# The last chunk tile by tile, row factors spread one chunk earlier, and two reordered pieces of preparation in a one-core transformer block

## The reference

```
h = layernorm(x)
C_q  = h @ Wq_d + bq_d            # 1024 -> 12
C_kv = h @ Wkv_d + bkv_d          # 1024 -> 4
q = (C_q @ W_qk + b_qk) by head   # 32 heads of 4
attn = softmax(q . C_kv / sqrt(4))
V = C_kv @ Wv_u + bv_u            # 32 heads of 32
x = x + (attn @ V) @ Wo + bo
x = x + layernorm(x) @ W.T + bias + LoRA(layernorm(x))
```

## Time and profile before

| | us |
|---|---|
| median of 3 runs | 2104.05 |
| lowest, highest | 2103.58, 2106.32 |
| time of the profiled execution | 2106.0 |
| span of its trace, first to last instruction | 2104.2 |
| TensorE busy | 1966.4 |
| ScalarE busy | 1959.2 |
| VectorE busy | 491.6 |
| GpSimd busy | 215.7 |
| mean granted TensorE clock, share of full | 0.989 |

### The profile page before, as it was taken

How to read it: one execution, slowest core, us unless ns; L and a number is a source line. 1 busy time by engine, 2 the same in 40 slices (tenths; PEclk the granted TensorE clock), 3 DMA queues, 4 the chain that set the end, 5 groups by cost and what they waited for, 6 DMA issues and landing times. The chain is left out here.

```text
span 2104.2 us, 36028 instructions
## 1 busy us (share of the span) xinstructions
PE 1966.4 (93%) x15041; PEld 713.3 (34%) x15041; DVE 491.6 (23%) x1213; ACT 1959.2 (93%) x2161; POOL 215.7 (10%) x220
## 2 busy tenths in 40 slices
PE   6868898999999999999999999999999999999999
PEld 3412222333333333333333333333333333333337
DVE  7812342211121111211111111212111111212115
ACT  3678999999999999999999999999999999999970
POOL 4700000000100001100100001100110001100021
PEclk9979999999999999999999999999999999999999
DMA  8452000000010000100010000100010000100010
GB/s 297 146 142 83 5 25 25 3 15 25 25 34 4 25 25 13 35 15 25 25 33 5 25 26 13 35 15 25 13 45 5 25 13 26 35 15 15 24 41 40
DMA packets 45663, 77.42 MB, mean 37 GB/s; under 512 B 15871, under 2 KB 29751, under 8 KB 45499
## 3 DMA queue, kind: packets, MB, share of 16 engines
q1 hardware_dynamic: 45498, 75.11, 10.6%
HBM read 51.23 MB, written 23.86 MB: 36 GB/s over the span
## 5 line engine op out<-in xcount | busy, mean ns | idle before, releaser
L610 ACT ACTIVATE probs<-ps 128x1024 f32<-128x1024 f32 x2048 | 1899.9, 1029 | 25.5 <-PE ps L842 14.9
L853 PE MATMUL ps<-probs,c_wide 128*32 128x512 f32 x8192 | 989.8, 601 | 0.0
L842 PE MATMUL ps<-q_in,key_t 27*128 27x512 bf16 x4096 | 405.4, 386 | 96.3 <-ACT probs L610 92.3
L899 PE MATMUL ps<-w_eff,xn_t 128*128 128x512 f32 x1344 | 394.3, 418 | 0.0
L853 PEld LDWEIGHTS ps<-probs,c_wide 128*32 128x32 f32 x8192 | 212.8, 108 | 427.0 <-issue 221.4
L842 PEld LDWEIGHTS ps<-q_in,key_t 27*128 27x128 bf16 x4096 | 103.0, 91 | 728.0 <-ACT probs L610 716.0
L1346 DVE SCALAR_TENSOR_TENSOR y<-ps,nw,y 128x512 f32<-128x512 f32 x64 | 48.0, 750 | 976.3 <-PE ps L899 967.3
L899 PEld LDWEIGHTS ps<-w_eff,xn_t 128*128 128x128 f32 x1344 | 228.2, 188 | 101.8 <-issue 69.8
L529 POOL TENSOR_TENSOR y<-y,ffn_bias 128x1024 f32<-128x1024 f32 x32 | 76.4, 2387 | 1358.3 <-DVEq L1367 1358.3
L524 POOL TENSOR_TENSOR y<-y,attn_bias 128x1024 f32<-128x1024 f32 x32 | 75.7, 2382 | 469.6 <-DMA y<-in_L_attn_x_dram 469.5
L541 ACT ACTIVATE area<-ps 128x512 f32<-128x512 f32 x64 | 37.3, 615 | 45.8 <-PE ps L641 45.8
(11 more groups left out here) (154 smaller groups left out, 591.3 us busy)
## 6 DMA issues: line engine op xcount, KB each, us to landing
y<-in_L_attn_x_dram SPq DMA_DIRECT2D x40, 512.0 KB, 4.0
out_dram<-y SPq DMA_DIRECT2D x32, 512.0 KB, 2.7
area<-in_L_attn_x_dram SPq DMA_DIRECT2D x16, 512.0 KB, 7.7
q_in<-q_parts SPq DMA_DIRECT2D x256, 27.0 KB
q_parts<-q_parts_sb SPq DMA_DIRECT2D x48, 128.0 KB, 2.6
xn<-in_L_attn_x_dram SPq DMA_DIRECT2D x8, 512.0 KB, 4.9
y<-in_L_attn_Wo_dram SPq DMA_DIRECT2D x1, 2048.0 KB, 8.3
xn<-in_L_attn_Wo_dram SPq DMA_DIRECT2D x1, 2048.0 KB, 14.4
```

Of the source, the lines that this page charges most:

```text
L610: nc.scalar.activation(probs[:, (c * STEPS + step) % PROBS, bass.ts(pair, 2 * N)], ps[:, 2 * (i % SCORE_SLOTS):2 * (i % SCORE_SLOTS) + 2, ...
L842: last = nc.tensor.matmul(ps[:, at, :], key_t[TILE * h:TILE * h + KEYS, bass.ts(b * KT + kt, P)], q_in[TILE * h:TILE * h + KEYS, g % 2, :] ...
L853: last = nc.tensor.matmul(ps[32 * h:32 * h + 32, SUMS, :], c_wide[:, b * KT + kt, at:at + 32], probs[:, (c * STEPS + step) % PROBS, bass.t ...
L899: last = nc.tensor.matmul(ps[:, SHARED, :], xn_t[:, t % 2, a, kb, :], w_eff[:, b, kb, bass.ts(half, N)], start=(kb + i == 0), stop=(kb == ...
```

## The change

Four edits, in the order of the time in which they act.

1. `spread_r(c)` moves to the end of its own chunk: on TensorE behind `turn_x(c, 7)`, on ScalarE directly behind the move of turned block 7, ahead of the value and query moves of chunk c-1. The multiplication by it stays where it is.
2. For the last chunk the queries are made ahead of the turned latents, and ScalarE writes `q_abs` first, then the values, then the queries. For the other chunks the order inside is the old one.
3. `turn_lora(m)` waits for `prep_ok` of m - 1 instead of m. VectorE moves both halves of lora_b first, and only then fills `lv`, in 8 copies of 32x16 instead of 32 copies of 32x4, and `bv_wide`.
4. The last chunk goes tile by tile: ScalarE copies the four tiles of the sums, each is turned into a bank of its own, normalized, turned back into a bank of its own, its high part copied by ScalarE and its low part subtracted by VectorE. ScalarE also takes the high halves of the turned y. The statistics of a tile come behind its split, the dense layer waits for each half of the turned y by itself, and the last tile is stored in two halves.

```
         # TensorE, stage 1
-                    if kb == 0 and c:
-                        spread_r(c - 1)
...
                     if kb == 6 and c:
-                        use_latents(c - 1, (c - 1) % 2)
+                        turn_latents(c - 1, (c - 1) % 2)
+                        queries(c - 1)
+                    if kb == KB - 1:
+                        spread_r(c)
...
-            use_latents(CHUNKS - 1, 1)
+            queries(CHUNKS - 1)
+            turn_latents(CHUNKS - 1, 1)
         # ScalarE, stage 1
-                    if kb == 1 and c:
-                        move_r(c - 1)
                     if kb == 4 and c:
                         move_latents(c - 1, (c - 1) % 2)
+                    if kb == KB - 1:
+                        move_r(c)
                     if kb == KB - 1 and c:
-                        move_products(c - 1, (c - 1) % 2, (c - 1) // 2)
+                        move_values(c - 1)
+                        move_q(c - 1, (c - 1) % 2, (c - 1) // 2)
+                        move_q_abs(c - 1)
         # preparation
             def turn_lora(m):
-                free_bank(m)
+                free_bank(m - 1)
...
+            dve.wait_ge(prep_ok, 1)
+            for odd in range(2):
+                for h in range(4):
+                    at = 16 * odd + L * h
+                    nc.vector.tensor_copy(lv[32 * h:32 * h + 32, odd::2, at:at + L], wv_t[32 * h:32 * h + 32, odd::2, :])
         # last chunk, ScalarE
+            act.wait_ge(pv_done, CHUNKS * STEPS)
+            for t in range(TT):
+                nc.scalar.activation(o_sb[:, bass.ts(t, P)], ps[:, SUMS, bass.ts(t, P)], ACT.Copy).then_inc(last_o, 1)
+            for t in range(TT):
+                act.wait_ge(last_back, t + 1)
+                nc.scalar.activation(o_t[:, 0, bass.ts(t, P)], ps[:, BACK_BANK[t], 0:P], ACT.Copy).then_inc(last_high, 1)
+            for t in range(TT):
+                act.wait_ge(ffn_ready, START + (p * TT + max(t - 1, 0)) * 2)
+                for u in range(2):
+                    act.wait_ge(t_ready, START + CHUNKS * KB + (p * TT + t) * 2 + u + 1)
+                    nc.scalar.activation(xn_t[:, t % 2, 0, 4 * u:4 * u + 4, :].rearrange("p a n -> p (a n)"),
+                                         ps[:, 4 + u, :], ACT.Copy).then_inc(y_high, 1)
         # last chunk, TensorE
+            for t in range(TT):
+                pe.wait_ge(last_o, t + 1)
+                nc.tensor.transpose(ps[:, t, 0:P], o_sb[:, bass.ts(t, P)], ident[:, :]).then_inc(last_turned, 1)
...
+            back_last(0)
+            back_last(1)
             project_last(0)
+            back_last(2)
+            back_last(3)
             project_last(1)
             turn_last(0)
             project_last(2)
         # last chunk, VectorE (each step for one tile)
+            norm_last(0)
+            norm_last(1)
+            split_last(0)
+            norm_last(2)
+            split_last(1)
+            norm_last(3)
+            split_last(2)
+            split_last(3)
...
             for t in range(TT):
-                ch = Chain(v_ln)
-                residual(p, t, (2 * (t % 2), 2 * (t % 2) + 1), ch)
+                residual_last(t)
                 if t:
                     add_dense(p, t - 1, 0, 6)
-                move_xn(p, t, (4, 5))
+                low_last(t)
+                ch = Chain(v_ln)
+                dve.wait_ge(y_ready, START + (p * TT + t + 1) * 2)
+                measure(ch, y, t)
                 finish(ch, t)
```

More of the change, by code:

```diff
@@ L250, in build_block @@
         out_done = [sem(f"out_done{t}") for t in range(TT)]
+        last_o = sem("last_o")
+        last_turned = sem("last_turned")
+        last_rec = sem("last_rec")
+        last_normed = sem("last_normed")
+        last_back = sem("last_back")
+        last_high = sem("last_high")
+        last_low = sem("last_low")
+        y_high = sem("y_high")
         block = ctx.enter_context(nc.Block())
@@ L455, in _ @@
             beside_attention(CHUNKS - 1, False, True)
+            for t in range(TT - 1):
+                store_out(CHUNKS - 1, t)
+            for half in range(2):
+                sp.wait_ge(ffn_moved, START + CHUNKS * UNITS - 1 + half)
+                sp.dma_start(out_t[CHUNKS * TT - 1][:, half * N:(half + 1) * N], y[:, TT - 1, half * N:(half + 1) * N]
+                             ).then_inc(out_done[TT - 1], 16)
             for t in range(TT):
-                store_out(CHUNKS - 1, t)
-            for t in range(TT):
-                sp.wait_ge(out_done[t], CHUNKS * 16)
+                sp.wait_ge(out_done[t], (CHUNKS + t // (TT - 1)) * 16)
         @block.gpsimd
@@ L678, in use_latents, with queries @@
                 last.then_inc(caug_ps, 1)
+            def queries(c):
                 pe.wait_ge(q_read, START + c)
@@ L1007, in _ @@
                 for half in range(2):
-                    pe.wait_ge(t_moved, START + CHUNKS * KB + (p * TT + t + 1) * 2)
                     if t:
                         pe.wait_ge(ffn_moved, START + (p * TT + t) * 2 - 1 + half)
+                    else:
+                        pe.wait_ge(last_low, TT)
                     for kb in range(KB):
+                        if half == 0 and kb % 4 == 0:
+                            pe.wait_ge(t_moved, START + CHUNKS * KB + (p * TT + t) * 2 + kb // 4 + 1)
                         if half == 1 and kb == KB // 2 and t < TT - 1:
@@ L1257, in _ @@
             ch.end()
-            dve.wait_ge(prep_ok, 1)
-            for g in range(G4):
-                for h in range(4):
-                    at = 16 * (g % 2) + L * h
-                    nc.vector.tensor_copy(lv[32 * h:32 * h + 32, g, at:at + L], wv_t[32 * h:32 * h + 32, g, :])
-            nc.vector.tensor_copy(bv_wide[:, :, 0:1], bv_col.unsqueeze(2)).then_inc(prep_ok, 1)
             for half in range(2):
@@ L1268, in _ @@
                                         ALU.mult, ALU.mult).then_inc(prep_ok, 1)
+            dve.wait_ge(prep_ok, 1)
[3 more added lines that the diff above has]
+                    nc.vector.tensor_copy(lv[32 * h:32 * h + 32, odd::2, at:at + L], wv_t[32 * h:32 * h + 32, odd::2, :])
+            nc.vector.tensor_copy(bv_wide[:, :, 0:1], bv_col.unsqueeze(2)).then_inc(prep_ok, 1)
             ch = Chain(v_set)
@@ L1388, in _, with norm_last @@
             p = CHUNKS - 1
-            move_o(p, 1)
-            norm_o(p, 1)
-            split_o(p)
-            dve.wait_ge(t_ready, START + CHUNKS * KB + p * UNITS)
+            dve.wait_ge(o_back, START + p)
+            def norm_last(t):
+                dve.wait_ge(last_turned, t + 1)
+                turned = ps[:, t, 0:P].rearrange("p (h m) -> p h m", h=4)[:, :, 0:4 * W5].rearrange("p h (g d) -> p h g d", d=W5)
+                nc.vector.reciprocal(recip[:, t, :, :], turned[:, :, :, L]).then_inc(last_rec, 1)
+                dve.wait_ge(last_rec, t + 1)
+                nc.vector.tensor_tensor(o_q[:, t, 64:128].rearrange("p (g h d) -> p h g d", h=4, d=L),
+                                        turned[:, :, :, 0:L], recip[:, t, :, :].unsqueeze(3).to_broadcast([P, 4, 4, L]),
+                                        ALU.mult).then_inc(last_normed, 1)
@@ new lines, in split_last @@
+            def split_last(t):
+                dve.wait_ge(last_high, t + 1)
+                nc.vector.tensor_tensor(o_t[:, 1, bass.ts(t, P)], ps[:, BACK_BANK[t], 0:P],
+                                        o_t[:, 0, bass.ts(t, P)].bitcast(F32), ALU.subtract).then_inc(last_low, 1)
+            norm_last(0)
+            norm_last(1)
+            dve.wait_ge(proj_ready, START + p * UNITS)
+            split_last(0)
+            norm_last(2)
+            split_last(1)
+            norm_last(3)
```

47 lines of the change are left out of this document (32 added, 15 removed).

## The result

| | before | after |
|---|---|---|
| median, us | 2104.12 (4 runs, 2103.58 to 2106.32) | 2087.63 (4 runs, 2087.39 to 2088.13) |
| profiled execution, us | 2106.0 | 2087.39 |
| span of its trace, us | 2104.2 | 2085.6 |
| mean granted TensorE clock | 0.989 | 0.996 |
| ScalarE idle ahead of exponentials | 25.5 | 19.1 |

The ratio of after to before is 0.992, with an interval of 0.9903 to 0.9937. The change gains 16.5 us by the medians, where 12.3 was forecast: 4.2 us short, outside the forecast's own 2089.8 to 2094 and at the very edge of the wide range, where rival A stood (2087.5). The direction was right.

What follows compares the result with a forecast made beforehand. ScalarE's exponentials were taken as the bound, so only time before, in holes of, or after them counts. 2106.0 - 5.6 - 2.0 - 4.1 - 0.6 = 2093.7 us profiled; median 2104.05 - 12.3 = 2091.8, range 2087.5 to 2097.

Steps and rivals of the forecast that it cites:

- rival A: Stage 1: the cast does not wait for GpSimd as read; 4.0 us gained in place of +0.3, 2087.5 us; chance 0.15.
- Place 1, the turned lora_b: Around 168 us: turning lora_b ahead of the lv copies removes ScalarE's 3.39 and 2.18 us holes, -5.6 us.
- rival B: Around 168 us: lv is late because copies cost by elements; times_wo stalls 3.8 us, 2097.4 us; chance 0.07.
- Place 2, stage 1: Loop of scales: copying the row factors earlier gains nothing, scale(5) +0.3 us, between -0.7 and +1.2.
- the cast waits for GpSimd's last split operation: Stage 1: VectorE's latents cast ends about 0.3 us after GpSimd's last split operation; 1.2 us gained, 1.6 given back.
- From scale(2) on VectorE is late by itself, and copying the factors earlier gives it nothing: Stage 1: VectorE's own chain of waits sets the 10.15 us between scales, so earlier row factors gain nothing there.
- From stage 1 to the first scores: Between scale(7) and attention: earlier factors and queries bring weigh to 107.4 from 109.45, -2.0 us (bounds -1.0 and -3.0).
- Rival E: Attention's start: TensorE stays at half clock longer, making the kernel slower than before; chance 0.02.
- Place 3: Last chunk's start: tile-by-tile work at assumed half clock starts the dense layer at about 2047.6, -4.1 us; 5 at full clock.
- Inside the dense part finer waits give nothing: Last chunk's dense matmuls: TensorE was continuous there, so finer waits gain nothing.
- C: Stage 1: GpSimd sets every chunk's loop, 0.25 us longer each; attention starts where it did, 2093.8 us; chance 0.12.
- D: Last chunk: its small pieces are dear, 2 us gained in place of 4.1, 2093.9 us; chance 0.08.

Runs made afterwards that it cites:

- With the split left out: GpSimd's split of the queries left out (second and third bf16 parts zero), in edit 1 alone and in the kernel before: 2097.72 and 2104.35 us, one run each.
- With edit 1 and without the split: Edit 1 alone on the kernel before, with GpSimd's split of the queries left out: 2097.72 us, one run.
- with the spare matmuls alone: The kernel before with four spare matmuls on TensorE in the last chunk's start: 2103.56 us, ratio 0.9993 (0.9984 to 1.0002).
- the spare matmuls at the start: The changed kernel with nine spare 128x512 f32 matmuls around attention's start, results never read: 2086.30 us, again 2085.88 against 2088.50 for the changed kernel.

## Why the prediction was wrong

The bound was read rightly: nearly everything gained lies ahead of the first exponential, in a hole of their row, or behind the last one. What failed is the clock: TensorE's half clock at the start of attention and of the last chunk was carried over unchanged, and the hole that it makes behind the first exponentials had a term of 0. One reading of the rows was wrong too. "The rest lies ahead of 130 us" made some 14 us of the 25.5 into idle time there, and the timeline has 3.35, the two holes; the waits view of before puts only 14.9 down to the scores. These 3.35 us were given no place in the sum. The steps one by one:

- **Place 1, the turned lora_b: right.** -5.6 forecast and traced; alone it gave 6.2 by the medians. With the 5.7 us that attention is ahead there, the forecast's 169.9 for lv is 164.2, and it was ready at 163.8. The copies cost per instruction, and rival B was never near. The 2.18 us of its second hole scatter in the kernel before (0.96 to 2.18 over the traces), so a term of one execution carried more than the other traces have; that edit 3 alone still gave 6.2 is no contradiction, since its interval goes from 3.8 to 8.2 us, and its trace had a fuller clock as well.
- **Place 2, stage 1: wrong in sign, small.** "Scale(5) +0.3" was measured as -0.95, less than a third of the way from there to rival A's -4.0. The step that failed is "the cast waits for GpSimd's last split operation". It waits only for the one that is running, gets in ahead of the next, and the VectorE operation behind it then waits. From scale(1) to scale(2) it is 10.56 us, where I had 11.8, and scale(2) came at 53.46, not 54.1. Scale(1) itself gained 0.62 of the forecast 1.2 between the two traces, and the rest of that is not the edit's. The `down` matmuls at 35.7 us took 1.47 us in the first trace of before and 1.89 after; in the second trace of before, of unchanged code, they took 1.90, and scale(1) came at 43.94, 1.04 behind the 42.90 of after. The section "Who interferes with whom" of the Trainium skill's "SBUF — State Buffer" has the later instruction blocked while the other holds the port; the traces agree, with that holder being one instruction (0.28 us behind 43.90), and it was I who had made it three.
- **"From scale(2) on VectorE is late by itself, and copying the factors earlier gives it nothing": half right.** With the split left out, the factors' copy appears as the wait for every scale. Up to scale(5) neither bound alone was worth more than 0.1 us a chunk. Behind it VectorE's list is shorter, and there the earlier factors did count: from scale(5) to scale(6) it is 9.02 us in the trace of edit 1 alone, where it was 10.11.
- **From stage 1 to the first scores: -2.0 against -3.8.** Scale(7) brought 2.1 of it, and the stretch from scale(7) to weigh 2.0. I had put the latter down to the order of the queries. The run without edit 2 shows that the order is worth 0.3 at full clock, and the trace of edit 2 alone that it was worth about 1 with the clock down behind 106 us. What made the old stretch long is that the queries (1.91 us) and the other matmuls ran at half clock: edit 3 alone, with the old order and the clock full, has 4.38 us from scale(7) to weigh, as edit 1 alone. In the old order TensorE waits 1.96 us for scale(7). With edit 1 that wait is 0.98, and the clock was still full from 104 to 108 us in all six traces with edit 1 and the split in place. Without edit 1 it was at half by 107 us in six traces of seven, and the seventh, edit 3 alone, took 12.05 us from scale(7) to the first exponential, as after the change. Two traces speak against too simple a rule. Edit 3 alone had the long wait (1.95 us) and kept the clock until 110. With edit 1 and without the split the wait was 0.98 and the clock fell all the same, between 100 and 102 us; it was 0.50 from 102 on, and the stretch from scale(7) to the first exponential took 12.49. What makes the clock fall in one execution and not in another stays open.
- **The clock at attention's start: a term of 0 that was -1.9.** Rival E asked only whether the clock could stay down longer. It came back earlier, between 118 and 120 us and not between 128 and 130, and one hole of two was gone. That I had priced such holes myself (1.9 us for a half-clock pair) and used it in one direction alone is the plainest mistake.
- **Place 3, -4.1 against -5.5: mis-sized by the assumed clock.** I wrote "TensorE is at half clock there now (0.50)" and "I assume the same", with 5 if it stayed up. In the one trace of this code in which it did fall the way takes 9.62 us, near the forecast's 9.9; otherwise 8.45. The granted clock was read as a property of the place. It was a property of how TensorE came to it: ahead of the projection it waited 0.81, 1.30 and 1.81 us before, and 0.49, 0.24 and 0.34 after, and with the spare matmuls alone the old start ran at 1.00. The edit was taking that idle time away.
- **"Inside the dense part finer waits give nothing": -1.0.** Before, the chain has pieces of 8.46 and 8.48 us for 36 matmuls beside one of 8.16; after, both such pieces are 8.16. That this is the wait for both halves fits edit 4's text, and the gain is in edit 4 alone, but no run tells it from the other parts of that edit.
- **The store, -0.6: right.**
- **The rivals.** A's reason did show in part: the cast met only one GpSimd operation, but the stretch did not vanish, it moved to the next operation. B, C, D and E did not show: lv was in time, the loop got shorter, the small pieces were cheaper than assumed, and the clock came back sooner.

Of the 6.3 us by which the traces exceed the forecast some 3.1 are the clock at attention's start and in the last chunk (1.9 + 1.2), 0.2 the last chunk's pieces, 1.8 the first exponential, of which the clock has its share too, 1.0 the dense part, 0.2 the rest. By the medians 4.2 are left, since the profiled execution of before stood nearly 2 us above its own.

Left open: how much of the 2 us of scatter between executions of before is the point at which the clock falls (no trace settles it; the second one, at 2105.86 us, had nearly the same half-clock stretches as the first), and whether edit 2 does anything for the second hole.

## What to carry to other kernels

When an edit takes an idle stretch away from TensorE, price what runs behind it at full clock as well as at the clock seen, and make the higher clock the likelier case: here it was full in five of six traces of the new last chunk, and worth 1.2 to 1.9 us at each of the two places. Where the engine still must idle at a seam between stages, a handful of matmuls into a bank nobody reads gave 2.6 us of 2088 by the medians. Before calling a wait worthless because another is right behind it, ask what each would be worth with both gone.

## What was unexpected in the hardware

- A VectorE operation that waits for GpSimd got in between two consecutive GpSimd operations: the cast at 43.51 ended 0.28 us behind one, while the next began at 43.96. The traces of edit 1 alone and of the second run of the changed kernel have the same (0.67 us for the cast, 1.62 and 1.63 for the operation behind it). It also goes the other way round. With the split left out, small GpSimd operations on 128x4 numbers, 0.20 us each, took 0.74 or 0.75 when they began beside VectorE's 0.75 us operation on bf16 and f32.
- TensorE's granted clock fell in some executions and not in others of the same program: at 2027 us in one of two with the spare matmuls at the start, and at 110 instead of 104 to 107 us in one of seven traces without edit 1. In the trace of edit 2 alone it fell at 106, was back at 1.00 from 110 to 112, and fell again.
- Stage 1 scatters by 0.9 us and more: scale(7) came at 101.28 and 101.64 us in two executions of the changed kernel, and at 100.73 with the same code up to there. In the six traces with the old stage 1 and the split it came between 102.49 and 104.17. Differences of a few tenths between two single traces, scale(5)'s -0.95 among them, are to be read with that.
